# Attention scores of two heads from two row tiles of 64, and a weighted sum that lags one head step

## What is computed

```python
q = layernorm(x) @ Wq                      # 128 x 1024
k, v = split(ctx @ Wkv)                    # 12544 x 1024 each
q, k, v = map(_split_heads, (q, k, v))     # 16 heads of 64
attn = softmax(einsum('bhid,bhjd->bhij', q, k) * 64 ** -0.5)
out = einsum('bhij,bhjd->bhid', attn, v)
x = x + out @ Wo + bo
# behind it: windowed attention, a mixture of 8 experts, attention over
# the context again, a scan, a mixture of 32 experts
```

## Time and profile before

| | |
|---|---|
| median of three runs | 1561.71 us |
| the profiled execution, its own time | 1565.5 us |
| its span, first to last instruction | 1563.8 us |
| TensorE busy | 1468.7 us, 94% |
| VectorE busy | 1242.0 us, 79% |
| ScalarE busy | 970.9 us, 62% |
| GpSimd busy | 604.6 us, 39% |
| mean granted TensorE clock | 0.971 |

### The profile page before, as it was taken

The page is one execution under the profiler, slowest core; times in us unless marked ns, Lnnn a source line. Parts: engine busy times, 40 slices in busy tenths (PEclk is TensorE's granted clock), DMA queues, the critical chain, the costliest instruction groups (busy, mean ns, idle before and its releaser), DMA issues. The chain is left out here.

```text
span 1563.8 us, 24194 instructions
## 1 busy us (share of the span) xinstructions
PE 1468.7 (94%) x8657; PEld 1303.5 (83%) x8657; DVE 1242.0 (79%) x2278; ACT 970.9 (62%) x1807; POOL 604.6 (39%) x519
## 2 busy tenths in 40 slices
PE   6999999999999999999999999999977989999479
PEld 5988998899889888988898889889865878888248
DVE  6888888888888888888888888888975356666764
ACT  4777777777777777777777777777651245555121
POOL 6334343434343434343434343433300256665330
PEclk9999999999999999999999999999997899999779
DMA  5000000000000000000000000000007122220600
GB/s 182 1 1 25 1 25 1 24 1 24 1 25 1 25 1 25 1 25 1 25 1 25 1 25 1 1 1 1 1 28 296 74 72 70 70 70 24 282 1 4
DMA packets 9099, 57.13 MB, mean 37 GB/s; under 512 B 2120, under 2 KB 2719, under 8 KB 7968
## 3 DMA queue, kind: packets, MB, share of 16 engines
q1 hardware_dynamic: 8992, 55.73, 9.6%
HBM read 55.60 MB, written 0.13 MB: 36 GB/s over the span
## 5 line engine op out<-in xcount | busy, mean ns | idle before, releaser
L314 POOL CAST V<-Vraw 128x512 fp32r<-128x512 f32 x189 | 115.8, 613 | 654.4 <-ACT Vraw L405 654.4
L369 ACT CAST K<-ps 64x448 fp32r<-64x448 f32 x448 | 236.4, 528 | 142.6 <-PE ps L532 133.1
L397 ACT ACTIVATE pT<-ps 128x896 fp32r<-128x896 f32 x224 | 206.3, 921 | 161.9 <-PE ps L558 161.7
L435 DVE TENSOR_TENSOR K<-ps,K 64x448 fp32r<-64x448 f32 x448 | 278.8, 622 | 13.3 <-ACT K L369 3.4
L493 DVE TENSOR_TENSOR pT<-ps,pT 128x896 fp32r<-128x896 f32 x224 | 244.6, 1092 | 31.9 <-ACT pT L397 8.3
L315 POOL TENSOR_TENSOR V<-Vraw,V 128x512 fp32r<-128x512 f32 x189 | 242.2, 1281 | 15.2
L443 DVE TENSOR_REDUCE nmx<-ps 128x1 f32<-128x896 f32 x224 | 242.2, 1081 | 0.0
L643 PEld LDWEIGHTS ps<-pT,V 128*128 128x128 f32 x1568 | 214.3, 189 | 17.0 <-DVE pT L493 7.5
L643 PE MATMUL ps<-pT,V 128*128 128x256 f32 x1568 | 222.5, 281 | 6.1 <-DVE pT L493 6.1
L379 ACT ACTIVATE prob<-ps,nm 128x896 f32<-128x896 f32 x224 | 224.3, 1001 | 0.0
L602 PE MATMUL ps<-ident,prob 128*128 128x128 f32 x1568 | 209.0, 274 | 0.0
(11 more groups left out here) (306 smaller groups left out, 2389.9 us busy)
## 6 DMA issues: line engine op xcount, KB each, us to landing
raw<-in_ctxT SPq DMA_DIRECT2D x14, 896.0 KB, 4.7
d_raw<-in_ctxT SPq DMA_DIRECT2D x14, 896.0 KB, 4.6
w<-in_w SPq DMA_DIRECT2D x2, 4096.0 KB, 16.8
wg<-in_wg SPq DMA_DIRECT2D x1, 4352.0 KB, 25.7
wu<-in_wu SPq DMA_DIRECT2D x1, 4352.0 KB, 16.8
wd<-in_wd SPq DMA_DIRECT2D x1, 4352.0 KB, 26.7
e_ea<-in_alog SPq DMA_DIRECT2D x1, 2048.0 KB, 7.3
wq<-in_wq SPq DMA_DIRECT2D x1, 1024.0 KB, 5.2
```

The source lines that it names most:

```text
L369: nc.scalar.copy(K[halves[s], slot, cols], ps[halves[s], piece_bank(p), 0:HK]).then_inc(sem("kh_ready"), 1)
L397: nc.scalar.activation(pT[:, :, 0, :], pT_ps, ACT.Copy).then_inc(sem("pTh_ready"), 1)
L435: ins = nc.vector.tensor_tensor(K[halves[1 - s], slot, cols], ps[halves[s], piece_bank(p), 0:HK], K[halves[s], slot, cols].bitcast(F32), A ...
```

## The change

- **Scores of two heads in one go.** `scores(pair)` runs at odd steps only, and makes heads u+1 and u+2: for each half of the chunk three products (qh·Kh, qh·Kl, ql·Kh), each as two matmuls over 64 rows, one on partitions 0 to 63 into `S[0]`, one on 64 to 127 into `S[1]`. Twelve matmuls for two heads in place of eight. The product low·low is no longer made. `qh` and `ql` hold each head once; K becomes Kh and Kl, each with both heads of a pair, so the high and the low parts of a piece are one operation of 128 partitions each; the copies that doubled `ql` are gone.
- **The weighted sum lags.** `weighted_sum(u-1)` stands at the end of step u, with two buffers for the turned probabilities; `turn_sums(u-2)`, `update_sums(u-2)` and `add_parts(u-1)` follow, the last now at the end of VectorE's step. `al` and `rs` have 8 columns.
- **Order.** Both maxima are taken in the odd step, `max_step(u+1)` right behind the low part of the turned probabilities, `max_step(u+2)` behind `den`. ScalarE copies `Vraw` ahead of the exponentials. AHEAD is 4; of eight steps the one without values is now 6 and no longer 7, and the context is split at step 14 of a chunk. The transposes wait for `pTl_ready` of the step before, the values for `o_added`.
- **Ends.** One piece less ahead of the loop; behind it one more turn, the last weighted sum and the last heads.
- Definitions of the norms, and when some tiles for later stages are reserved, only move in the text.

```diff
-    AHEAD = 5
+    AHEAD = 4
-    v_steps = [u for u in range(steps - HG) if u % HG < NT]
-    VS = len(v_steps)
+    V_AT = (0, 1, 2, 3, 4, 5, 7)
+    v_steps = [u for u in range(steps - HG) if u % HG in V_AT]
...
-        qh = sb("qh", [P, H0, P], F32R, keep)
-        ql = sb("ql", [P, H0, P], F32R, keep)
-        K = sb("K", [P, 2 * RING, CK], F32R, keep)
+        qh = sb("qh", [P, PAIRS, P], F32R, keep)
+        ql = sb("ql", [P, PAIRS, P], F32R, keep)
+        Kh = sb("Kh", [P, RING, CK], F32R, keep)
+        Kl = sb("Kl", [P, RING, CK], F32R, keep)
...
-        pT = sb("pT", [P, NT, 2, P], F32R, keep)
+        pT = [sb(f"pT{i}", [P, NT, 2, P], F32R, keep) for i in range(2)]
...
-        al = sb("al", [P, 4], F32, keep)
-        rs = sb("rs", [P, 4], F32, keep)
+        al = sb("al", [P, 8], F32, keep)
+        rs = sb("rs", [P, 8], F32, keep)
...
                 for u in range(steps - HG):
-                    if u % HG < NT:
+                    if u in v_steps:
                         split_values(v_steps.index(u))
-                    if u % H0 == H0 - 1 and u // H0 + 2 < chunks:
+                    elif u % H0 == H0 - 2 and u // H0 + 2 < chunks:
                         split_context(u // H0 + 2)
...
-                for s in range(2):
-                    for d in range(2):
-                        nc.scalar.activation(by_pair(qh)[halves[d], :, s, :], q_ps(ps)[halves[s]], ACT.Copy,
-                                             scale=SCALE).then_inc(sem("qh_ready"), 1)
+                nc.scalar.activation(qh[:, :, :], q_ps(ps), ACT.Copy, scale=SCALE).then_inc(sem("qh_ready"), 1)
 
                 def high_parts(p):
                     act.wait_ge(sem("piece_done"), p + 1)
                     if p // 2 >= RING:
-                        act.wait_ge(sem("scores_done"), 2 * (p // 2 - RING) + 2)
-                    for s in range(2):
-                        slot, cols = piece_of(p, s)
-                        nc.scalar.copy(K[halves[s], slot, cols], ps[halves[s], piece_bank(p), 0:HK]).then_inc(
-                            sem("kh_ready"), 1)
+                        act.wait_ge(sem("scores_done"), p // 2 - RING + 1)
+                    slot, cols = piece_of(p)
+                    nc.scalar.copy(Kh[:, slot, cols], ps[:, piece_bank(p), 0:HK]).then_inc(sem("kh_ready"), 1)
 
                 def exp_step(u):
-                    par, h, b = (u // H0) % 2, u % H0, u % 4
+                    par, h, b = (u // H0) % 2, u % H0, u % 8
                     act.wait_ge(sem("max_done"), u + 1)
-                    if u >= 4:
-                        act.wait_ge(sem("u_added"), u - 3)
+                    if u >= 8:
+                        act.wait_ge(sem("u_added"), u - 7)
...
-                    if p == 2:
-                        for s in range(2):
-                            act.wait_ge(sem("ql_ready"), s + 1)
-                            nc.scalar.copy(by_pair(ql)[halves[1 - s], :, s, :],
-                                           by_pair(ql)[halves[s], :, s, :].bitcast(F32)).then_inc(sem("ql_doubled"), 1)
...
                 for u in range(steps):
                     act.wait_ge(sem("p_turned"), u + 1)
-                    nc.scalar.activation(pT[:, :, 0, :], pT_ps, ACT.Copy).then_inc(sem("pTh_ready"), 1)
-                    if u + 1 < steps:
-                        exp_step(u + 1)
+                    nc.scalar.activation(pT[u % 2][:, :, 0, :], pT_ps, ACT.Copy).then_inc(sem("pTh_ready"), 1)
                     if u in v_steps:
                         j = v_steps.index(u)
                         act.wait_ge(sem("v_done"), NT + j + 1)
                         if j >= 2:
                             act.wait_ge(sem("v_split"), j - 1)
                         nc.scalar.copy(Vraw[:, j % 2, :], ps[:, 6, :]).then_inc(sem("vraw_ready"), 1)
+                    if u + 1 < steps:
+                        exp_step(u + 1)
                     if u + AHEAD < steps:
                         high_parts(u + AHEAD)
...
                 def low_parts(p):
-                    dve.wait_ge(sem("kh_ready"), 2 * p + 2)
-                    for s in range(2):
-                        slot, cols = piece_of(p, s)
-                        ins = nc.vector.tensor_tensor(K[halves[1 - s], slot, cols], ps[halves[s], piece_bank(p), 0:HK],
-                                                      K[halves[s], slot, cols].bitcast(F32), ALU.subtract)
-                    ins.then_inc(sem("kl_ready"), 1)
+                    dve.wait_ge(sem("kh_ready"), p + 1)
+                    slot, cols = piece_of(p)
+                    nc.vector.tensor_tensor(Kl[:, slot, cols], ps[:, piece_bank(p), 0:HK], Kh[:, slot, cols].bitcast(F32),
+                                            ALU.subtract).then_inc(sem("kl_ready"), 1)
...
-                    dve.wait_ge(sem("scores_done"), u + 1)
+                    dve.wait_ge(sem("scores_done"), u // 2 + 1)
...
-                    h, b = u % H0, u % 4
-                    dve.wait_ge(sem("p_turned"), u + 2)
+                    h, b = u % H0, u % 8
+                    dve.wait_ge(sem("p_turned"), u + 3)
...
                         max_step(0)
-                        max_step(1)
+                max_step(1)
                 for u in range(steps):
-                    h, b = u % H0, u % 4
-                    if u >= 1:
-                        add_parts(u - 1)
-                        if u - 1 + AHEAD < steps:
-                            low_parts(u - 1 + AHEAD)
+                    h, b = u % H0, u % 8
+                    if 1 <= u and u - 1 + AHEAD < steps:
+                        low_parts(u - 1 + AHEAD)
                     dve.wait_ge(sem("pTh_ready"), u + 1)
-                    nc.vector.tensor_tensor(pT[:, :, 1, :], pT_ps, pT[:, :, 0, :].bitcast(F32),
+                    nc.vector.tensor_tensor(pT[u % 2][:, :, 1, :], pT_ps, pT[u % 2][:, :, 0, :].bitcast(F32),
                                             ALU.subtract).then_inc(sem("pTl_ready"), 1)
-                    if u >= 1:
-                        update_sums(u - 1)
+                    if u % 2 == 1 and u + 1 < steps:
+                        max_step(u + 1)
+                    if u >= 2:
+                        update_sums(u - 2)
                     if u >= H0:
                         dve.wait_ge(sem("u_added"), u - H0 + 1)
                     nc.vector.tensor_scalar(den[:, h:h + 1], den[:, h:h + 1], al[:, b:b + 1],
                                             rs[:, b:b + 1], ALU.mult, ALU.add)
-                    if u + 2 < steps:
+                    if u % 2 == 1 and u + 2 < steps:
                         max_step(u + 2)
-                    m = (u - (steps - H0)) // 2 - 1
-                    if u > steps - H0 and u % 2 == 0:
-                        scale_sums(m)
+                    if u >= 1:
+                        add_parts(u - 1)
+                    if u >= steps - H0 + 3 and u % 2 == 1:
+                        scale_sums((u - (steps - H0) - 3) // 2)
+                update_sums(steps - 2)
                 add_parts(steps - 1)
                 update_sums(steps - 1)
                 scale_sums(PAIRS - 1)
...
-                def scores(u):
-                    h, b = u % H0, u % 2
+                def scores(pair):
+                    m, slot = pair % PAIRS, pair % RING
                     for half in range(2):
-                        keys = K[:, key_slot(u), half * HK:(half + 1) * HK]
-                        nc.tensor.matmul(S[b][:, half, :], qh[:, h, :], keys, start=True, stop=False)
-                        mm = nc.tensor.matmul(S[b][:, half, :], ql[:, h, :], keys, start=False, stop=True)
+                        keys, n = slice(half * HK, (half + 1) * HK), 0
+                        for w, x in ((qh, Kh), (qh, Kl), (ql, Kh)):
+                            for s in range(2):
+                                mm = nc.tensor.matmul(S[s][:, half, :], w[halves[s], m, :], x[halves[s], slot, keys],
+                                                      start=(n == 0), stop=(n == 2))
+                            n += 1
                     mm.then_inc(sem("scores_done"), 1)
 
...
+                def weighted_sum(u):
+                    h, g = u % H0, u // HG
+                    pe.wait_ge(sem("pTl_ready"), u + 1)
+                    if u >= 1:
+                        pe.wait_ge(sem("o_added"), u)
+                    if h % HG == 0:
+                        if g == 0:
+                            pe.wait_ge(sem("first_vl"), NT)
+                        else:
+                            pe.wait_ge(sem("v_split"), NT * g)
+                    for k in range(NT):
+                        mm = nc.tensor.matmul(OT_ps, V[g % 2][:, k, h % HG, :],
+                                              pT[u % 2][:, k, :, :].rearrange("p a q -> p (a q)"),
+                                              start=(k == 0), stop=(k == NT - 1))
+                    mm.then_inc(sem("pv_done"), 1)
...
```

(98 more changed lines are left out.)

11 lines of the change are left out of this document (removed).

## The result

The changed kernel took 1557.09 us (median of 8, 1551.67 to 1558.09) beside 1563.41 us for the kernel before: a ratio of 0.995, interval 0.9935 to 0.9965. The forecast was 1546.2, about 15.5 us less than before; the medians differ by 6.3 us, and the interval of the ratio spans 5.5 to 10. Two later measurements of the same kernel, each beside the kernel before, gave 0.9922 (0.9905 to 0.9939) and 0.9938 (0.9918 to 0.9958), 12 and 11 us.

The account below looks back on a forecast made before the run. TensorE's stream was taken to bound the first stage to 98%. 13 chunks −6.5 and the ends −9 gave −15.5 on 1565.5, so 1550.0, or 1546.2 us against the median; range 1522 to 1598.

Parts of the forecast that it names:

- What bounds the kernel: First stage: TensorE's stream bounds it to 98%, with VectorE and ScalarE hidden.
- the scores' streams: Scores of a head pair on TensorE: from 8 streams, 1.64 us, to 6, 1.31 us with two loads per stream.
- S: Time of a pair's scores on TensorE: 1.31 us plus 0.29 for switches, 1.60; bounds 1.23 and 2.85.
- The odd step: Step that makes a pair's scores: S + 4.38 us, at the least 5.82; forecast 5.98, 0.05 of it a wait.
- VectorE's queue: Odd step: `add_parts(u-1)` ends at A + 5.31, the turn wants it at A + 5.64; hidden by 0.2 to 0.3 us.
- The even step without values: Step without scores or values: TensorE would need 2.93 us, but the turn waits for `add_parts` behind `den`: 3.24 us.
- A: Start of ScalarE's copy of the turned probabilities, 1.07 us behind the opening of a step where nothing waits.
- The ends: Start −5 us, steps 208 to 222 −6, extra turn and weighted sum behind the loop +2; together −9, bounds −3 and −12.
- the partial overlap: Rival on the scores: a pair of streams takes a quarter more than one, 0.256 us; S 1.83, +8, 1570 us; chance 0.15.
- the binding chain: Rival on odd steps: the chain binds and S, at most 1.44, no longer matters; −32, 1529 us; chance 0.12.
- the streams one after the other: Rival on the twelve matmuls of `scores(pair)`: 64-row streams don't overlap; S 2.75, +104, 1666 us; chance 0.13.
- the waiting loads: Rival on the scores: a tile's next weights can't load while it streams; S 2.17, +44, 1610 us; chance 0.07.

Follow-up runs that it names:

- e1: Changed kernel with the weighted sum ahead of the piece in even steps without values: 1556.03 us, ratio 0.9932 to the kernel before.
- e3: Changed kernel with the weighted sum ahead of the piece in steps without values and the `u_added` wait ahead of the fifth transpose only: 1547.24 us, ratio 0.9882.
- again_changed: Changed kernel measured once more without edits, beside the kernel before; the two such repeats took 1554.11 and 1553.91 us, ratios 0.9922 and 0.9938.
- e9_start_order: Kernel before with the first two heads' scores moved right behind the fourth piece, ahead of the fifth piece and first value tiles: 1563.35 us, ratio 0.9991.

## Why the forecast was wrong

Step by step, as it was put:

- **What bounds the kernel, and the scores' streams: right.** Two matmuls on different row tiles run as one stream. The two loads per stream don't show: 0.205 a pair, where 0.218 was allowed. The ways in and out: the switch out was priced at 0.19 from the earlier trace rows and measured 0.19, in part by luck: the matmuls over one row there stand behind a wait of 0.65, and a restart alone costs about 0.10, which these rows can't tell from a switch. The switch in, taken as 0.10 with bounds 0 and 0.2, is 0.20, the upper bound. The Trainium skill, TensorEngine Tiling (Array Packing), Key Properties, has the rule that a change of the tiling mode drains TensorE; the rows agree, with a late start at both ends, 0.20 and 0.19. The two errors, 0.08 too much for the loads and 0.10 too little for the switch in, nearly cancel, which is luck: S 1.63 for 1.60. The difference cost nothing, for the odd step had 0.05 of waiting in the forecast that took it up.
- **The odd step: right.** 5.96 measured, 5.98 forecast. The exponential does not quite hold it: in the step shown it is done at 612.59, and the transposes start at 612.67, where the weighted sum's stream ends.
- **VectorE's queue: right in the odd step.** The turn waits for no `osb`; the even step with values takes 4.35 for 4.33.
- **The even step without values: wrong, and this is the term that failed.** 3.55 for 3.24, so 0.62 us a chunk and 8.1 us in 13. With the even steps (6 × 0.02) and the odd ones (8 × −0.02) that is 0.58 a chunk, 7.5 in 13, and the first chunk was 0.63 longer than the others (81.51 for 80.88, its second step waits 0.63 for the exponential). Together 8.2, about the 7.9 by which the chunks missed. I took `den` and then `add_parts` as what is late, and followed only the turn. The change also puts `update_sums(u-2)` behind the low part of the turned probabilities of step u, and the seven transposes of step u+1 wait for it (`u_added`): by the prediction's own figures it ends at A + 1.96 + 0.34 = A + 2.30, and with 1.07 from the opening to A, 0.05 and up to 0.10 of restart the step is 3.42 to 3.52. The number could be had from the earlier trace rows; the wait was in the diff. The piece's wait for the low keys was not in the sum at all. `e1` to `e3` show both: with the piece's wait alone covered the step stays at 3.55, with the wait for `u_added` alone put later it is 3.35, with both 3.30. So of the 0.31 that were missing the wait for `update_sums` is 0.20, the low keys are 0.05, and 0.06 is left, where the transposes wait for the exponential.
- **The ends: near in sum, by luck, and wrong in one part.** Start −5.2 for −5, last steps −4.8 for −6. Behind the last step I forecast +2 for the extra turn and sum, and it was −2.3. The granted clock makes the difference. The table of stretches (length, busy us and count of PE, PEld, DVE, ACT and POOL, granted clock, DMA share, GB/s), for the kernel before, steps 220 to 222 in part and then the end of the stage:

```profile
1155.00:1169.47 14.47, 8.94 (x50) 7.59 (x50) 8.80 (x21) 6.75 (x13) 0.00 (x0) 0.88 0.00 0
1169.47:1181.20 11.73, 10.69 (x40) 7.69 (x38) 3.83 (x11) 1.66 (x3) 0.00 (x0) 0.71 0.01 1
```

and for the changed kernel:

```profile
1146.50:1160.87 14.37, 8.23 (x66) 6.89 (x64) 11.35 (x29) 8.44 (x17) 0.00 (x0) 1.00 0.00 1
1160.87:1170.32 9.45, 8.35 (x46) 6.37 (x46) 4.97 (x16) 1.78 (x4) 0.00 (x0) 1.00 0.00 0
```

Before, the last steps and the end have the clock at 0.88 and 0.71: it is granted at 0.50, the lower level of 1.2 GHz, from about 1162.8 to 1166.2 and again from about 1169.6 to 1176.4. In this trace of the changed kernel it stays at 2.4. TensorE's rows show what it costs, read from start to start, in the kernel before

```profile
1162.38 1.56 PE L643 MATMUL ps<-pT,V 128*128 128x256 f32 x7 [1.32 <-DVE pT L493]
...
1164.59 1.70 PE L602 MATMUL ps<-ident,prob 128*128 128x128 f32 x7
...
1168.54 1.09 PE L643 MATMUL ps<-pT,V 128*128 128x256 f32 x7 [2.13 <-DVE pT L493]
...
1171.18 1.22 PE L631 MATMUL ps<-brow,ones 1*128 1x256 f32 x2
...
1172.33 3.78 PE L568 MATMUL ps<-wo,oT 128*128 128x256 f32 x8
...
1175.55 1.58 PE L643 MATMUL ps<-pT,V 128*128 128x256 f32 x7
```

and in the changed one

```profile
1161.69 1.07 PE L553 MATMUL ps<-pT,V 128*128 128x256 f32 x7
...
1162.69 0.69 PE L632 MATMUL ps<-brow,ones 1*128 1x256 f32 x2
...
1163.31 1.99 PE L566 MATMUL ps<-wo,oT 128*128 128x256 f32 x8
...
1165.14 0.27 PE L540 MATMUL ps<-ident,osb 128*128 128x128 f32 x1
```

The eight matmuls over `wo` take 3.22 us for 1.83 (1172.33 to 1175.55, 1163.31 to 1165.14), the two ahead of them 1.15 for 0.62, the transposes that open step 223 1.36 for 0.79, the last weighted sum 1.42 for 0.91: together 3.0 us. The weighted sum that the change puts here costs 1.0 (1161.69 to 1162.69), not 2; the two nearly make the −2.3. In steps 221 and 222 the lower clock took another 1.1 of the kernel before: a weighted sum of 1.37 us where 0.94 is usual, transposes of 1.50 for 0.79.

Ahead of the first fall TensorE had waited twice for 1.32 us, ahead of the second for 2.13. But in the changed kernel it waited 1.80 and 1.66 us in these steps without a fall, and was busy for no larger share of the stretch before (8.23 of 14.37 us, 8.94 of 14.47 in the other). And in `again_changed` the same kernel had its fall in step 218. So why the clock fell where it did is not settled. In all three traces of the changed kernel, and of all edits of it, the stretch from step 223 to the end of the stage took 9.0 to 9.1 us, and 11.0 in `e9_start_order`, which has the loop of the kernel before and a clock of 0.73 there.

The sum by the trace is then −11.5 for −15.5: the chunks 8 us short, the tail 4 us better, the start and the last steps within 1.2. That it came as near as this is luck: about 4 us of what the ends won are the clock's, which no term of the forecast had. Of the rivals, the partial overlap, the binding chain, the streams one after the other and the waiting loads are excluded by the rows of L533. The forecast's own case was the true one, and its gain was sized at twice or more what the first measurement gave, and a third above the two later ones. One sum of the rivals is off: loads that wait for their tile, at +44, would come to 1606 us against the same median as the others, not 1610.

## What to carry to other kernels

When work is taken off a stream that is full, list for every step of the pattern, the shortest above all, each semaphore that its next instruction waits for, with the time at which that semaphore comes; the latest decides, and removing it only brings out the next (here the step took 3.55 us with the wait for the low keys covered, 3.35 with the sums' update out of the way, 3.30 with both, and then the exponential held it). A wait belongs ahead of the first instruction that needs it, not ahead of the group: moving one by four transposes brought 4 to 6 us. And row tiles of 64, at the price measured here, pay only if they save more than 0.4 us of streams per visit, or lighten another engine, as they did here.

## What the hardware showed

- Two matmuls over 64 rows each, on different row tiles and different PSUM banks, start within about 0.01 us of each other and run as one, 0.205 us a pair, with the two fp32r weight loads of the next pair hidden behind it.
- Matmuls on one tile are overtaken by later ones in program order on the other tile: with three of one, then three of the other, the chip paired them all the same, and time didn't change (1553.96 us). The Trainium skill, TensorE: Matmul & The Clock Gate, The mechanism, lets only loads pass a matmul, and keeps matmuls in order; the measurement differs and decides.
- A switch from 128 rows to 64 and back takes 0.20 and 0.19 us, as much as one stream of 448 columns each; twice as many switches cost 42 us in 104 steps, 0.40 a pair (0.39 by the traces).
